# Gated delta layer: merge products on quarters of the array, output and squares as moving operand

## The chip, the cores and the metric

One core of one Trainium2 chip runs one program of eight layers. Its engines are TensorE (PE in the rows; its weight loads are PEld), VectorE (DVE), ScalarE (ACT), GpSimd (POOL) and SyncE (SP), each with its own queue of instructions in program order. They meet at semaphores. The metric is the device time of one execution in microseconds.

## The reference, cut to what matters

The change touches the first layer alone, a gated delta rule with 16 heads (DK = 64, DV = 128), here on 8 batches of 256 tokens, D = 128. T and B of the arrays are set by the inputs.

```python
def _L0_attn_ref(x, w_q, w_k, w_v, w_a, w_b, w_g, w_out, A_log, dt_bias, conv_q, conv_k, conv_v, norm_w):
    q, k, v = x @ w_q, x @ w_k, x @ w_v
    beta = sigmoid(x @ w_b) * 2.0
    g = -exp(A_log) * softplus(x @ w_a + dt_bias)
    q, k, v = (silu(causal_conv4(a, w)) for a, w in ((q, conv_q), (k, conv_k), (v, conv_v)))
    q, k = (a * rsqrt(sum(a * a, -1) + 1e-6) for a in (q, k))          # per head
    def step(S, inp):                                                  # per token and head
        S = S * exp(g_t)
        delta = (v_t - k_t @ S) * b_t
        S = S + outer(k_t, delta)
        return S, (q_t * DK ** -0.5) @ S
    rms = o * rsqrt(mean(o * o, -1) + 1e-5)
    y = rms * norm_w * silu(x @ w_g)
    return y @ w_out                                                   # 2048 -> 128
```

The rest of the network (window attention, Pluecker attention, flash attention, two Mamba scans, four feed-forward blocks) is the same in both kernels.

## The kernel before, in words

`gated_delta` works in chunks of 128 tokens. A quad is one batch with one group of four heads, both chunks (c = 0, 1); there are 8 x 4 = 32 quads. The token recurrence within a chunk becomes a triangular system, whose inverse is built block by block: GpSimd inverts the 16x16 diagonal blocks (`invert`), then three levels of merges double the block, l = 0 (16), l = 1 (32), l = 2 (64). Each merge is two products on TensorE for each chunk, `merge_y` (L1888) and `merge_t` (L1900), four matmuls each, with a copy or masking between them on VectorE (`step_4`, `step_5`, `step_6`) and a copy back on ScalarE (`copy_t`) behind. In between stand small transposes on VectorE (`turn_blocks`, `turn_64`).

The order is written out by hand. Four quads are in flight: `step(x0, x1, x2, x3)` of each engine does the first part of quad x0 (projections, convolution, norms, masked products), pieces of x1, the merges, the solve and the outputs of x2, and the gating and output product of x3. `quads` runs four steps in the body of a loop over the batches, with steps ahead of it and behind it unrolled.

Names used below. `project(x0, n)` (L1821): n = 0 is q, 1 is k, 2 and 3 are v; q and the first half of v go to PSUM bank 4, k and the second half of v to bank 5. ScalarE takes each out of PSUM with the last tap (`tap3`, L2063), VectorE adds the other three taps (`conv`, L2314, six instructions). `sum_squares` (L1838): eight matmuls whose stationary operand is a 128x128 piece of the squares and whose moving operand is `halves` with 2 columns; the sums come out with tokens on partitions, in bank 6. `norms` (L2368 to L2378) on VectorE makes the powers out of them. `out(x3, c)` (L1981): four matmuls per chunk with y as the stationary operand; `add_y` (L2430) on VectorE adds the result from bank 5 into `block_out`. The next projection into bank 5 waits for that add (semaphore `done`).

In the rows each fp32 matmul shows twice ("x16" is eight matmuls), a transpose once. In a step VectorE's order is: masks of level 0, `add_y(x3, 0)`, `conv(x0, 0)`, `step_5`, `conv(x0, 1)`, `turn_64`, `step_6(x2, 0)`, `conv(x0, 2)`, `norms(x0)`, `add_y(x3, 1)`, `step_6(x2, 1)`, `conv(x0, 3)`, then the masked products, `subtract_memory`, `turn_16` and `add_o`, which the next quad's first merge waits for.

## Time and profile before

| | |
|---|---|
| median of 3 runs | 5082.28 us (5075.35 to 5099.08) |
| profiled execution | 5070.0 us, span of the profile 5068.0 us |
| mean granted TensorE clock | 0.896 |
| busy in the span | PE 4077.8 us (80%), DVE 3765.4 (74%), POOL 2812.8 (56%), PEld 2568.3 (51%), ACT 2407.9 (48%) |
| first layer, L1888 (first merge products) | 1536 instructions of 128x64, 188.3 us busy |
| L1900 (second merge products) | 1536 of 128x64, 210.1 us busy |
| L1838 (sums of squares) | 512 of 128x2, 67.7 us busy |
| L1981 (output product) | 512 of 128x128, 75.1 us busy |

The busy times are unions of an engine's instructions. In the rows below, a time ahead of an instruction group is its start in microseconds from the span's start, followed by how long the group lasts; the end of the last matmul of a group is modelled and reaches some 0.2 us past the start of the next. A bracket tells how long the engine sat idle before the group and what ended that. The granted clock is 1.00 at 2.4 GHz and 0.50 at 1.2 GHz.

### The profile page before, as it was taken

To read this page: it belongs to the slowest core of one execution; us is meant where nothing else is said; L and a number is where in the kernel's file an instruction comes from. 1 tells how busy PE (TensorE), PEld (TensorE's weight loads), DVE (VectorE), ACT (ScalarE), POOL (GpSimd) and SP (SyncE) were. 2 spreads that over 40 slices of the span, in tenths; PEclk is the share of its full clock that TensorE was granted. 3 is DMA by queue.
4 is the path that set the end of the run, shared out by engine and by line. 5 is a ranking of instruction groups with operands and counts; after the bars stand their busy time and mean duration, and the time that the engine had idled before them with its cause. 6 is when DMAs were issued, how large, how long until landed. Compare 5 with 4: busy or idle time off the path is not lost. (4 is left out here: it accounts for less than half of the span.)

```text
span 5068.0 us, 74799 instructions
## 1 busy us (share of the span) xinstructions
PE 4077.8 (80%) x19653; PEld 2568.3 (51%) x19773; DVE 3765.4 (74%) x6424; ACT 2407.9 (48%) x4932; POOL 2812.8 (56%) x2705
## 2 busy tenths in 40 slices
PE   5999999999768668667879965688888758888884
PEld 4777777777646546456447742233333323333332
DVE  5676776676567468456138866899999869999995
ACT  3555555555334234222236642566666436666661
POOL 2555555555344144043013330799999529999991
PEclk8999999999877778778999986899999979999997
DMA  1000000000000000000000000000000000000000
GB/s 49 8 8 8 8 8 8 8 7 8 17 0 0 8 13 0 12 1 23 0 17 1 0 13 10 0 0 0 0 0 0 8 0 0 0 0 0 0 0 13
DMA packets 90077, 33.20 MB, mean 7 GB/s; under 512 B 78032, under 2 KB 86112, under 8 KB 88928
## 3 DMA queue, kind: packets, MB, share of 16 engines
q1 hardware_dynamic: 89824, 30.16, 2.5%
q8 instruction: 119, 1.95, 0.2%
q14 instruction: 134, 1.10, 0.1%
HBM read 24.87 MB, written 5.24 MB: 6 GB/s over the span
## 5 line engine op out<-in xcount | busy, mean ns | idle before, releaser
L2970 POOL TENSOR_TENSOR dBx<-dtx,b_row 128x1024 f32<-128x1024 f32 x512 | 1220.4, 2384 | 3.9 <-ACT b_row L2936 3.9
L3004 DVE TENSOR_TENSOR_SCAN h<-banks,dBx 128x1024 f32<-128x1024 f32 x512 | 1168.6, 2283 | 18.1 <-ACT banks L2930 18.1
L2888 PE MATMUL banks<-hc,ident 128*128 128x512 f32 x2048 | 964.6, 594 | 0.0
L2930 ACT ACTIVATE banks<-dt,A 128x510 f32<-128x510 f32 x1024 | 661.7, 682 | 3.6 <-DVE h L3004 3.6
L2936 ACT ACTIVATE b_row<-banks 128x512 f32<-128x512 f32 x512 | 305.9, 597 | 574.1 <-PE banks L2872 574.1
L2888 PEld LDWEIGHTS banks<-hc,ident 128*128 128x128 f32 x2048 | 388.8, 190 | 272.2 <-issue 246.8
L3012 DVE TENSOR_TENSOR hc<-h,banks 128x768 f32<-128x768 f32 x512 | 478.6, 935 | 10.3 <-ACT c_row L2941 6.8
L2872 PE MATMUL banks<-bc_lo,selectors 128*128 128x512 bf16 x1024 | 391.3, 382 | 82.9 <-POOL b_row L2959 73.9
L2979 POOL TENSOR_TENSOR hc<-h,c_row 128x256 f32<-128x256 f32 x512 | 377.0, 736 | 54.5 <-ACT c_row L2941 28.7
L2871 PE MATMUL banks<-bc_hm_c,selectors 128*128 128x512 bf16 x506 | 195.1, 386 | 185.3 <-DVE hc L3012 185.0
L155 POOL MEMSET minus_half<- 128x16 f32 x13 | 1.5, 113 | 520.8 <-POOLq L234 178.8
L2871 PEld LDWEIGHTS banks<-bc_hm_c,selectors 128*128 (+1 forms) x512 | 49.2, 96 | 434.0 <-issue 433.8
L2314 DVE SCALAR_TENSOR_TENSOR v_featmajor<-banks,taps,v_featmajor 128x255 f32<-128x255 f32 (+2 forms) x384 | 167.3, 477 | 130.5 <-ACT v_featmajor L2063 120.0
L2256 POOL TENSOR_TENSOR out_factors<-out_norms,exponents 128x4 f32<-128x4 f32 x64 | 64.5, 1008 | 320.4 <-DVE out_norms L2423 320.4
L821 POOL TENSOR_TENSOR weighted<-probs,f 128x1024 f32<-128x1024 f32 x64 | 120.8, 1904 | 214.8 <-DVE f L872 203.9
L1900 PE MATMUL banks<-inv_turned,steps 128*128 128x64 f32 x1536 | 210.1, 287 | 5.2 <-DVE steps L2339 4.2
L195 PE MATMUL banks<-ident,norm 128*128 128x128 f32 x176 | 45.4, 452 | 209.6 <-DVE norm L165 164.1
L1900 PEld LDWEIGHTS banks<-inv_turned,steps 128*128 128x128 f32 x1536 | 199.2, 203 | 19.5 <-DVE steps L2339 8.7
L1888 PE MATMUL banks<-inv,A_turned 128*128 128x64 f32 x1536 | 188.3, 277 | 24.1 <-issue 19.5
L1888 PEld LDWEIGHTS banks<-inv,A_turned 128*128 128x128 f32 x1536 | 183.2, 196 | 30.9 <-issue 30.9
L2872 PEld LDWEIGHTS banks<-bc_lo,selectors 128*128 (+1 forms) x1024 | 99.6, 97 | 184.0 <-issue 167.0
L2314 DVE SCALAR_TENSOR_TENSOR qk<-banks,taps,qk 128x255 f32<-128x255 f32 (+2 forms) x384 | 167.0, 476 | 23.2 <-ACT qk L2063 12.6
(411 smaller groups left out, 9057.8 us busy)
## 6 DMA issues: line engine op xcount, KB each, us to landing
delta_blocks<-A_turned SPq DMA_DIRECT2D x256, 8.0 KB, 1.5
inv_turned<-delta_blocks SPq DMA_DIRECT2D x256, 8.0 KB, 1.8
blocks<-delta_blocks SPq DMA_DIRECT2D x32, 64.0 KB, 2.1
delta_blocks<-blocks_inv SPq DMA_DIRECT2D x32, 64.0 KB, 1.9
wh<-in_l1f_wh SPq DMA_DIRECT2D x1, 2048.0 KB, 7.6
wqkv<-in_l0f_wqkv SPq DMA_DIRECT2D x2, 768.0 KB, 4.3
residual<-in_x SPq DMA_DIRECT2D x1, 1024.0 KB, 4.7
wv<-in_l0a_wv SPq DMA_DIRECT2D x1, 1024.0 KB, 7.5
```

Of the source, the lines that this page charges most:

```text
L1888: i = mm(k.bank[c][:, h * 64:(h + 1) * 64].rearrange("p (n s) -> p n s", s=s), AT[:, hg, c, h, :], Tm[:, hg % 2, c, h, :].rearrange("p (n ...
L1900: i = mm(k.bank[2 + c][:, h * 64:(h + 1) * 64].rearrange("p (n s) -> p n s", s=s), (step4, step5, step6)[l][:, c, h, :], TT[:, hg % 2, c, ...
L2314: i = stt(out=dst[:, back:], in0=k.bank[4 + n % 2][:, m * T:(m + 1) * T - back], scalar=taps[:, first + m, j:j + 1], in1=dst[:, back:], op ...
L2871: nc.tensor.matmul(k.bank[bank], onto_all(sel[:, 0, bass.ds(n, 1)]), mem[part][:, cols], start=True, stop=False)
L2872: nc.tensor.matmul(k.bank[bank], onto_all(sel[:, which, bass.ds(n, 1)]), mem["lo"][:, cols], start=False, stop=True).then_inc(q[ready], 1)
L2888: i = nc.tensor.matmul(k.bank[e], k.ident[:], hc[:, s, e, :], start=False, stop=False)
L2930: i = nc.scalar.activation(a3[:, :, 1:], d3[:, :, 1:], ACT.Exp, scale=mem["A"][:, e, bass.ds(n, 1)])
L2936: nc.scalar.activation(bsb[:, s, :], k.bank[BBANK], ACT.Copy).then_inc(q["bsb_ready"], 1)
L2970: nc.gpsimd.tensor_tensor(dBx[:, s % NS], dtx[:, :, bass.ds(c * SCH, SCH)], across(bsb[:, s % NS, :], SE), ALU.mult).then_inc(q["dbx_ready ...
L2979: nc.gpsimd.tensor_tensor(hc[:, s % 2, :, DC:], h[:, s % NS, :, DC:], across(csb[:, s % 2, :], SE), ALU.mult).then_inc(q["hcp_ready"], 1)
L3004: v.tensor_tensor_scan(flat(h[:, s % NS]), flat(k.banks[:, at:at + SE, :]), flat(dBx[:, s]), 0.0, ALU.mult, ALU.add).then_inc(q["scanned"], 1)
L3012: v.tensor_tensor(hc[:, s % 2, :, 0:DC], h[:, s, :, 0:DC], across(k.bank[CBANK][:, 0:DC], SE), ALU.mult).then_inc(q["hc_ready"], 1)
```

## The change

Four things. (1) Merge levels 1 and 2 use a part of the array: level 1 two products of 64x64 weights on opposite quarters for each head, with 32 moving columns, level 2 one product of 64x64 weights with 64 columns. The copies on ScalarE shrink to the part that is written, at level 1 in two instructions. (2) The output product has `wout` as the stationary operand and y of both chunks (256 columns) as the moving one. It is done once per quad, summed feature-major over the four quads of a batch in `acc`, then turned by two transposes (`turn_out`) and copied to `block_out` (`copy_out`). (3) `sum_squares` has `halves` as the stationary operand (128 x 8) and the squares as the moving one (256 columns), four matmuls that accumulate. ScalarE copies the 8 x 256 sums (`copy_norms`), and two transposes of TensorE turn them (`turn_norms`); `norms` on VectorE reads the same place as before. (4) The clearing of `block_out` and the filling of two tiles with the identity go, one clearing comes.

The core of the diff:

```diff
-    d["l0a_halves"] = f(row // 64 == np.arange(2)[None, :])
+    d["l0a_halves"] = np.concatenate([f(np.arange(8)[None, :] == 2 * n + row // 64) for n in range(4)], 1)
...
+        def halves_of(a, s):
+            a = a.rearrange("p (n two s) -> p n two s", two=2, s=s)
+            return a[:, :, 0, :], a[:, :, 1, :]
...
                     elif n == 1:
-                        wait(pe, "done", 2 * (qa - LAG - 1) + 1)
+                        if hg == NG - 1:
+                            wait(pe, "yout", b)
...
                     else:
-                        wait(pe, "done", 2 * (qa - LAG))
+                        wait(pe, "done", qa - LAG)
                         wait(pe, "conv", 4 * qa + 2)
...
                     wait(pe, "sq", qa + 1)
                     wait(pe, "Dexp", 2 * qa + 2)
+                    for n in range(4):
+                        i = mm(k.bank[6][0:8, 256:512], halves[:, n, :], sq[:, n, :], start=n == 0, stop=n == 3)
+                    i.then_inc(q["ssfm"], 1)
+
+                def turn_norms(a):
+                    qa = a[0]
+                    wait(pe, "sscp", qa + 1)
+                    pe.sem_inc(q["through_pe"], 1)
                     for c in range(TPB):
-                        for n in range(4):
-                            i = mm(k.bank[6][:, c * 8 + n * 2:c * 8 + n * 2 + 2], sq[:, n, c * P:(c + 1) * P], halves[:],
-                                   start=True, stop=True)
+                        i = tr(k.bank[6][:, c * 8:c * 8 + 8], ssf[:, c * P:(c + 1) * P], k.ident[0:8, 0:8])
                     i.then_inc(q["ssps"], 1)
...
                     for h in range(HG):
-                        i = mm(k.bank[c][:, h * 64:(h + 1) * 64].rearrange("p (n s) -> p n s", s=s), AT[:, hg, c, h, :],
-                               Tm[:, hg % 2, c, h, :].rearrange("p (n two s) -> p n two s", two=2, s=s)[:, :, 0, :],
-                               start=True, stop=True)
+                        cols = slice(h * 64, (h + 1) * 64)
+                        t = Tm[:, hg % 2, c, h, :]
+                        if l == 0:
+                            i = mm(k.bank[c][:, cols].rearrange("p (n s) -> p n s", s=s), AT[:, hg, c, h, :], halves_of(t, s)[0],
+                                   start=True, stop=True)
+                        elif l == 1:
+                            for n in range(2):
+                                r = slice(64 * n, 64 * n + 64)
+                                i = mm(k.bank[c][r, h * 64 + 32 * n:h * 64 + 32 * n + 32], AT[r, hg, c, h, r], t[r, 64 * n:64 * n + 32],
+                                       start=True, stop=True)
+                        else:
+                            i = mm(k.bank[c][64:128, cols], AT[0:64, hg, c, h, 64:], t[0:64, 0:64], start=True, stop=True)
                     i.then_inc(q["Yps"], 1)
...
-                def out(a, e, c):
+                def out(a, x1, e):
                     qe, b, hg = e
-                    wait(pe, "yT", 2 * qe + c + 1)
...
+                    wait(pe, "yT", 2 * qe + 2)
+                    if a is not None:
+                        wait(pe, "conv", 4 * a[0] + 2)
...
                     for h in range(HG):
-                        i = mm(k.bank[5][:, 0:D], yT[:, c, h, :], wout[:, hg * HG + h, :], start=h == 0, stop=h == HG - 1)
+                        i = mm(k.bank[5][:, 0:T].rearrange("p (c t) -> p c t", c=TPB), wout[:, hg * HG + h, :], yT[:, :, h, :],
+                               start=h == 0, stop=h == HG - 1)
                     i.then_inc(q["fin"], 1)
+
+                def turn_out(x1, b):
+                    wait(pe, "done", (b + 1) * NG)
...
+                    for t in range(TPB):
+                        i = tr(k.bank[5][:, t * P:(t + 1) * P], acc[:, t * P:(t + 1) * P], k.ident[:])
+                    i.then_inc(q["yturn"], 1)
...
-                    if x3:
-                        out(x1, x3, 0)
+                    if x3 and x3[2] == 0 and not first(x3):
+                        turn_out(x1, x3[1] - 1)
...
                     if x3:
-                        out(x0, x3, 1)
+                        out(x0, x1, x3)
...
                     if x0:
+                        turn_norms(x0)
                         turn_k(x0)
                         project(x0, 3)
...
+                def copy_norms(a):
+                    qa = a[0]
+                    wait(act, "ssfm", qa + 1)
+                    fn(ssf[:], k.bank[6][0:8, 256:512], ACT.Copy).then_inc(q["sscp"], 1)
...
-                    s = (16, 32, 64)[l]
-                    fn(odd(TT[:, hg % 2, c], s), packed(2 + c, s), ACT.Copy).then_inc(q["TTc"], 1)
+                    if l == 1:
+                        t = packed(2 + c, 32)
+                        fn(TT[0:32, hg % 2, c, :, 32:64], t[0:32, :, 0, :], ACT.Copy)
+                        i = fn(TT[64:96, hg % 2, c, :, 96:128], t[64:96, :, 1, :], ACT.Copy)
+                    else:
+                        i = fn(TT[0:64, hg % 2, c, :, 64:128], packed(2 + c, 64)[0:64, :, 0, :], ACT.Copy)
+                    i.then_inc(q["TTc"], 1)
...
-                def add_y(e, c):
+                def add_y(e):
                     qe, b, hg = e
-                    wait(dve, "fin", 2 * qe + c + 1)
+                    wait(dve, "fin", qe + 1)
+                    y = k.bank[5][:, 0:T]
+                    if hg == 0:
+                        i = vv.tensor_copy(acc[:], y)
+                    else:
+                        i = tt(acc[:], y, acc[:], ALU.add)
+                    i.then_inc(q["done"], 1)
+
+                def copy_out(b):
+                    wait(dve, "yturn", b + 1)
                     dve.sem_inc(q["through_dve"], 1)
-                    y = k.Y[:, bass.ds(b * TPB + c, 1), :].rearrange("p a d -> p (a d)")
-                    tt(y, k.bank[5][:, 0:D], y, ALU.add).then_inc(q["done"], 1)
+                    vv.tensor_copy(k.Y[:, bass.ds(b * TPB, TPB), :].rearrange("p a d -> p (a d)"), k.bank[5][:, 0:T]).then_inc(q["yout"], 1)
```

`merge_t` is changed as `merge_y` is; the rest of the diff repeats these edits in waits and steps.

How the order changes on TensorE from the last merge level to the masked products, in the body of the loop. Before:

```order
L1888 MATMUL banks<-inv,A_turned 128x64 x8
L1900 MATMUL banks<-inv_turned,steps_3 128x64 x4
L1838 MATMUL banks<-halves,squares 128x2 x8
L1924 MATMUL banks<-v,inv_turned 128x128 x4
L1914 MATMUL banks<-wg,x_batch 128x512
L1845 MATMUL banks<-ident,qk 128x128 x2
L1821 MATMUL banks<-norm_featmajor,wv 128x256 x2
```

And of the change, with the semaphores that each waits for:

```order
L1938 MATMUL banks<-inv_turned,steps_3 64x64 x3
L1750 REGISTER_ALU
L1848 MATMUL banks<-squares,halves 8x256 [waits Dexp_3,sq_3]
L1848 MATMUL banks<-squares,halves 8x256 x3
L1750 REGISTER_ALU
L1962 MATMUL banks<-v,inv_turned 128x128 [waits vtok_3,TTc_3]
L1962 MATMUL banks<-v,inv_turned 128x128 x3
L1750 REGISTER_ALU
L1952 MATMUL banks<-wg,x_batch 128x512 [waits conv_3,xb_3]
L1856 MATMUL banks<-ident,norms_featmajor 128x8 [waits sscp_3]
L1856 MATMUL banks<-ident,norms_featmajor 128x8
L1862 MATMUL banks<-ident,qk 128x128 x2
```

The squares are now the moving operand, and two transposes stand behind the gate projection (L1952), where the norms on VectorE get their input.

VectorE between the transposes of the 32-blocks and the convolution of q (`qk`), before:

```order
L2346 TENSOR_TENSOR inv_turned<-banks,inv_turned 128x16x16 [waits TTps_3] x2
L2324 STREAM_TRANSPOSE inv<-inv_turned 32x8x32 x4
L1748 REGISTER_ALU
L2430 TENSOR_TENSOR block_out<-banks,block_out 128x128 [waits fin_3]
L1748 ISA
L2314 SCALAR_TENSOR_TENSOR qk<-banks,taps,qk 128x255 [waits tap3_3]
L2314 SCALAR_TENSOR_TENSOR qk<-banks,taps,qk 128x255
```

And of the change:

```order
L2406 TENSOR_TENSOR inv_turned<-banks,inv_turned 128x16x16 [waits TTps_3] x2
L2384 STREAM_TRANSPOSE inv<-inv_turned 32x8x32 x4
L1750 ISA
L2374 SCALAR_TENSOR_TENSOR qk<-banks,taps,qk 128x255 [waits tap3_3]
L2374 SCALAR_TENSOR_TENSOR qk<-banks,taps,qk 128x255
```

The add, which waits for TensorE's first output product (`fin`), no longer stands ahead of the convolution. The other add of a step keeps its place behind the norms and is now 256 wide; once a batch, `copy_out` stands where the first one stood.

## Rows read from the trace of the kernel before

**Rows 1.** Page, granted clock in 40 slices of the span, tenths

```profile
PEclk8999999999877778778999986899999979999997
```

**Rows 2.** Stretches of the first layer: length, busy time (instructions) by engine, clock

```profile
core 0: us, PE busy (x) PEld busy (x) DVE busy (x) ACT busy (x) POOL busy (x), PEclk, DMA share, GB/s
107.67:1266.54 1158.87, 1057.70 (x6941) 863.15 (x6941) 811.35 (x2322) 594.84 (x1303) 622.87 (x1243) 0.92 0.06 8
704.34:745.45 41.11, 38.16 (x240) 31.02 (x241) 28.07 (x81) 20.53 (x46) 21.59 (x43) 0.88 0.05 8
745.45:785.20 39.75, 36.73 (x241) 30.14 (x241) 28.06 (x81) 20.55 (x46) 21.60 (x43) 0.91 0.05 8
826.56:864.89 38.33, 35.01 (x242) 28.65 (x241) 28.18 (x80) 20.09 (x45) 21.61 (x43) 0.96 0.06 8
810.68:823.31 12.63, 8.97 (x67) 6.91 (x66) 11.89 (x35) 6.18 (x16) 6.12 (x6) 0.97 0.04 4
```

**Rows 3.** The same view, stretches around the sums of squares

```profile
126.40:129.80 3.40, 3.40 (x12) 2.42 (x12) 1.36 (x8) 1.14 (x4) 0.00 (x0) 0.51 0.19 17
841.90:846.30 4.40, 4.40 (x42) 4.40 (x41) 3.04 (x7) 2.37 (x5) 3.06 (x10) 1.00 0.00 0
846.70:850.10 3.40, 3.40 (x11) 2.26 (x11) 1.71 (x8) 1.14 (x4) 1.35 (x2) 0.52 0.16 21
1245.90:1252.70 6.80, 6.80 (x24) 5.30 (x24) 2.10 (x11) 1.53 (x5) 3.80 (x4) 0.50 0.16 22
```

**Rows 4.** TensorE in order of time, one quad: start, length, instructions, idle before

```profile
797.97 1.08 PE L1821 MATMUL banks<-norm_featmajor,wv 128*128 x4
799.55 1.16 PE L1981 MATMUL banks<-wout,y_featmajor 128*128 128x128 f32 x8 [0.50 <-DVE qk L2314]
803.17 1.90 PE L1838 MATMUL banks<-halves,squares 128*128 128x2 f32 x16
...
810.45 1.14 PE L1859 MATMUL banks<-qk 64*128 64x256 f32 x8
811.52 1.13 PE L1940 MATMUL banks<-weighted,k_tokens 128*128 128x256 f32 x4
...
816.35 1.16 PE L1924 MATMUL banks<-v,inv_turned 128*128 128x128 f32 x8
818.21 0.60 PE L1872 MATMUL banks<-ident,v_featmajor 128*128 128x128 f32 x4
...
823.04 2.04 PE L1829 MATMUL banks<-g_masked,tri 128*128 128x512 f32 x2 [3.03 <-issue]
```

**Rows 5.** VectorE in order of time, the same quad

```profile
789.90 1.78 DVE L2324 STREAM_TRANSPOSE inv<-inv_turned 32x256 f32<-32x256 f32 x4
792.49 0.29 DVE L2430 TENSOR_TENSOR block_out<-banks,block_out 128x128 f32 x1 [0.80 <-PE banks L1981]
792.70 2.75 DVE L2314 SCALAR_TENSOR_TENSOR qk<-banks,taps,qk 128x255 f32<-128x255 f32 x6
...
805.11 0.17 DVE L2368 TENSOR_SCALAR norms<-banks 128x16 f32<-128x16 f32 x1 [0.30 <-PE banks L1838]
...
806.52 0.29 DVE L2430 TENSOR_TENSOR block_out<-banks,block_out 128x128 f32 x1
...
810.68 2.76 DVE L2314 SCALAR_TENSOR_TENSOR v_featmajor<-banks,taps,v_featmajor 128x255 f32<-128x255 f32 x6 [3.42 <-ACT v_featmajor L2063]
```

**Rows 6.** ScalarE in order of time, the same quad

```profile
790.41 0.84 ACT L2063 ACTIVATE qk<-banks,taps 128x256 f32<-128x256 f32 x2 [3.14 <-PE banks L1821]
```

**Rows 7.** TensorE in order of time, flash attention: weights of 64 columns

```profile
2657.14 1.15 PE L703 MATMUL banks<-weighted_keymajor,v 128*64 128x128 f32 x16
```

**Rows 8.** Stretches of the Mamba layer (columns as in rows 2)

```profile
3143.70:3147.10 3.40, 2.71 (x7) 0.35 (x5) 2.99 (x6) 0.00 (x0) 0.00 (x0) 1.00 0.00 0
3150.50:3158.00 7.50, 7.50 (x11) 2.82 (x10) 0.00 (x0) 1.97 (x1) 0.00 (x0) 0.50 0.00 0
```

**Rows 9.** Groups by shape, TensorE, 3143.7 to 3147.1: count | busy us, mean ns

```profile
L2712 PE MATMUL banks<-xc,w_xp 128*8 128x512 f32 x4 | 1.9, 593 | 0.0
```

**Rows 10.** TensorE in order of time, 3150.5 to 3158: 8 active rows

```profile
3149.98 9.01 PE L2718 MATMUL banks<-dt_low,w_dt 8*128 8x512 f32 x11
```

More of the change, by code:

```diff
@@ L1716, in gated_delta @@
         tri, hide, ident = p.sb("tri", [P, 2, P]), p.sb("hide", [P, P], BF16), p.sb("ident_bf16", [P, P], BF16)
-        merge, halves, taps = p.sb("merge", [P, 64]), p.sb("halves", [P, 2]), p.sb("taps", [P, 32, 4])
+        merge, halves, taps = p.sb("merge", [P, 64]), p.sb("halves", [P, 4, 8]), p.sb("taps", [P, 32, 4])
         expo = p.sb("exponents", [P, 2 * 2 * HG])
@@ L1735, in gated_delta @@
         gate, yT = p.sb("gate", [P, TPB, HG, DV]), p.sb("y_featmajor", [P, TPB, HG, P])
+        ssf = p.sb("norms_featmajor", [8, T])
+        acc = p.sb("batch_out_featmajor", [P, T])
         sqo, os_, of = p.sb("out_squares", [P, HG, DV]), p.sb("out_norms", [P, TPB, HG]), p.sb("out_factors", [P, TPB, HG])
@@ L1739, in gated_delta @@
                  "xb", "conv", "T16", "Ystep", "TT4", "T32", "T64", "ss", "sp", "AP", "w1", "O1", "osum", "done", "rD", "zeroed",
-                 "inverted", "passed", "passing", "rn", "wd", "y", "there", "back", "through_pe", "through_pool", "through_act", "through_dve")
+                 "inverted", "passed", "passing", "rn", "wd", "y", "yturn", "yout", "ssfm", "sscp", "there", "back", "through_pe", "through_pool", "through_act", "through_dve")
         q = {n: p.sem(n) for n in names}
@@ L1761, in quads, with first @@
                 step(*[at(B - 1, NG + s - n) if n > s else None for n in range(DEPTH)])
+        def first(x):
+            return isinstance(x[1], int) and x[1] == 0
         def even(a, s):
@@ L1898, in merge_t @@
                         wait(pe, "TTc", 4 * qe + c + 1)
+                    pe.sem_inc(q["through_pe"], 1)
                     for h in range(HG):
-                        i = mm(k.bank[2 + c][:, h * 64:(h + 1) * 64].rearrange("p (n s) -> p n s", s=s),
-                               (step4, step5, step6)[l][:, c, h, :],
-                               TT[:, hg % 2, c, h, :].rearrange("p (n two s) -> p n two s", two=2, s=s)[:, :, 1, :],
-                               start=True, stop=True)
+                        cols = slice(h * 64, (h + 1) * 64)
+                        t = TT[:, hg % 2, c, h, :]
+                        if l == 0:
+                            i = mm(k.bank[2 + c][:, cols].rearrange("p (n s) -> p n s", s=s), step4[:, c, h, :], halves_of(t, s)[1],
+                                   start=True, stop=True)
+                        elif l == 1:
+                            for n in range(2):
+                                r = slice(64 * n, 64 * n + 64)
+                                i = mm(k.bank[2 + c][r, h * 64 + 32 * n:h * 64 + 32 * n + 32], step5[r, c, h, r],
+                                       t[r, 64 * n + 32:64 * n + 64], start=True, stop=True)
+                        else:
+                            i = mm(k.bank[2 + c][0:64, cols], step6[64:, c, h, 0:64], t[64:, 64:], start=True, stop=True)
                     i.then_inc(q["TTps"], 1)
@@ L1910, in project_gate @@
                     else:
-                        wait(pe, "yT" if c == 0 else "done", 2 * qe)
+                        if c == 0:
+                            wait(pe, "yT", 2 * qe)
+                        else:
+                            wait(pe, "done", qe)
                     wait(pe, "xb", b + 1)
@@ L1964, in turn_y @@
                         wait(pe, "conv", 4 * a[0] + 1)
+                    else:
+                        wait(pe, "yT", 2 * qe + 1)
                     for h in range(HG):
@@ L2174, in step @@
                         copy_t(x2, 2, 0)
+                    if x0:
+                        copy_norms(x0)
+                    if x2:
                         scale_z(x2, 0)
@@ L2287, in start @@
                 def start():
-                    vv.memset(k.Y[:], 0.0)
                     vv.memset(Tm[:], 0.0)
@@ L2291, in start @@
                     vv.memset(tmp[:], 0.0)
-                    for s in (step5, step6):
-                        vv.tensor_copy(s[:].rearrange("p c h t -> p (c h) t"), across(k.ident[:], TPB * HG))
+                    vv.memset(step5[:], 0.0)
                     dve.drain()
@@ L2444, in step @@
                         turn_blocks(x2, "T32")
-                    if x3:
-                        add_y(x3, 0)
+                    if x3 and x3[2] == 0 and not first(x3):
+                        copy_out(x3[1] - 1)
                     if x0:
@@ L2460, in step @@
                     if x3:
-                        add_y(x3, 1)
+                        add_y(x3)
                     if x2:
@@ L2477, in _ @@
                 quads(dve, step, start)
+                copy_out(B - 1)
 def delta_prologue(k, p, m):
```

17 lines of the change are left out of this document (9 added, 8 removed).

## The prediction

> **What bounds the kernel now.** I read the page's slices first: in the first quarter of the span TensorE's clock stands at 8 to 9 tenths, not at full speed [rows 1]. Then the busy time by stretches [rows 2]. The first layer (the gated delta rule, the only code touched) runs from about 100 to 1305 us in a steady cadence, 29 quads from 107.67 to 1266.54, or 39.96 us each. A quad is the stretch from one start of the first merge product (L1888) to the next. TensorE is busy 91% of it, VectorE 70%.
>
> The same view of three quads shows what makes one quad longer than another. At a granted clock of 0.96 a quad takes 38.33 us, at 0.91 39.75, at 0.88 41.11 [rows 2]. With only the levels 1.0 and 0.5, a mean of 0.96 over 38.33 us is 2 x 0.04 x 38.33 = 3.1 us at the low level; the others are 7.2 and 9.9 us. So 1 us at the low level costs (41.11 - 38.33) / (9.9 - 3.1) = 0.41 us. At 0.92 the mean quad has 6.4 us of it, which costs 2.6 us.
>
> Finer stretches say where the clock is lost [rows 3]. From 841.9 to 846.3 TensorE does not idle at all, yet it issues matmuls of 64 columns (merge products) and of 2 columns (sums of squares); right behind, from 846.7 to 850.1, the clock is 0.52. A low stretch follows this place in all 29 quads, of 3.4 us in 21 of them (the first is at 126.4) and of twice that in 8 (the last is at 1245.9), 4.4 us in the mean. The remaining 2 us per quad lie at the loop's end and at the first merge.
>
> Last, I followed one quad in order of time on TensorE, VectorE and ScalarE [rows 4 to 6]. TensorE waits 0.50 us before the output product at 799.55, for the convolution of k on VectorE, which could not start before the convolution of q had ended (792.70 + 2.75). The quad's second half hangs on VectorE: from 810.68 (the last convolution) to 823.31 it is busy 11.9 of 12.63 us [rows 2]. So whatever starts the last convolution earlier or later moves the quad's end by as much.
>
> **The change, part by part**, as time per quad at the full clock unless said.
>
> (a) Output product. Of two products of 4 matmuls (16 instructions, since each fp32 matmul counts twice in the rows) one of 8 instructions with 256 columns is left. 256 columns cost 0.215 us each (x4 in 1.08 less the last one's tail of 0.2 [rows 4]), so 1.72 us for 2 x 0.98. That alone is 0.2 us. More matters what stood behind it: VectorE waited 0.80 us for the first product (792.49), added, and only then began to convolve q at 792.70. Its input was ready at 791.25 (790.41 + 0.84 on ScalarE [rows 6]) and VectorE free at 791.68 (789.90 + 1.78 [rows 5]). Without the add the convolution starts at about 791.7: both convolutions and all that follows them come 1.0 us earlier. Bounds 0.7 and 1.1.
>
> (b) Merge products on quarters. Level 2: 64 weight columns in place of 128. The nearest row with 64 weight columns takes 16 instructions in 1.15 us [rows 7], 0.06 each after the tail, against 0.11 (x16 in 1.90). Level 1 has twice the instructions, in pairs on opposite quarters. The nearest pairs are the 64-row ones: 8 of 256 columns in 1.07 us (810.45 to 811.52), so two run beside each other. I take 0.5 us for a group of 0.88; bounds 0.44 and 0.88 (no overlap). Of this little reaches the end: level 1 stands between waits for VectorE (the 32-block transposes end at 791.68, the convolution of q after it), and goes into those waits. Level 2, first three groups: 3 x 0.4 = 1.2 us less.
>
> Each visit to a quarter or half of the array costs something at its edges. The four pairs of 810.45 should take 4 x 0.215 = 0.86 and take 1.07: 0.21 per visit, in and out. The Trainium skill, TensorEngine Tiling, Key Properties, says that changing the mode drains the engine; by that alone I would count the visits as here, and the 0.21 agrees. Visits added on the path: level 2, the sums, and the turn of the norms, 0.6 us.
>
> (c) Sums of squares. Before, 16 instructions of 2 columns took 1.90 us less tail, bound by 128-column weight loads. Now 8 instructions with 8 weight columns and 256 moving columns: 8 x 0.215 = 1.72. No gain in time. Together (a) to (c) on TensorE, from the end of k's convolution to the end of the sums: before 5.4 us (799.5 to 803.17 + 1.76), now 1.7 + 0.1 + 1.5 (level 2 with its wait for VectorE's copy) + 0.1 + 1.7 = 5.2. So only the 1.0 us of (a) stands.
>
> (d) The turned sums, the part that costs. The norms on VectorE (L2368 and after) now need a copy on ScalarE (hidden behind the solve and the gate projection, 1.86 us from 816.35 to 818.21) and two transposes that stand behind both. VectorE's chain from the first norm instruction to the add behind it is 1.41 us (805.11 to 806.52 [rows 5]); the add of 256 columns lies between 0.29 (one of 128, 806.52) and 0.46 (one step of the convolution, 2.75 / 6), I take 0.42. And the last projection of v waits for that add ("done"), since it overwrites bank 5. Before, the add ended at 806.81 and the projection came later anyway; now it is late next: transposes 0.3 (four take 0.6, row of 818.21) and their edges 0.2, mode change out of the sums 0.1, handovers 0.15, chain 1.41, add 0.42, exposed first weight load 0.1, less the 0.33 of the k transposes that now hide in the wait = 2.3 us. Behind the waiting projection stand on TensorE the last merge, the k·k products and all that follows; ScalarE's tap and VectorE's last convolution wait for it. Bounds 1.5 (part hidden) and 2.7. TensorE idles about 1.6 us there, a new wait.
>
> (e) The clock. The low stretch behind the sums should go. The mamba layer has both cases [rows 8 to 10]: four matmuls of 512 columns with only 8 weight columns, all 128 rows active, at clock 1.00, and no fall after them; and eleven of 512 columns with 8 active rows, back to back, at 0.50. [...] Gain 4.4 x 0.41 = 1.8 us; bounds 0 and 1.8. But the new wait of (d), with two tiny transposes before it and quarter products behind it, makes a thin stretch of its own two microseconds later. Before the loop's end TensorE waited 3.03 us (823.04), and the clock fell to about half behind it (x2 of 512 columns in 2.04 us; at 0.215 for 256 they would take 0.86, 1.02 with the tail). I give a fall there two chances in three, at 0.9 us (it covers less of the path): +0.6. Bounds 0 and 2.8 (two low stretches). The Trainium skill, TensorE: Matmul & The Clock Gate, section "Why this matters for your kernels", asks for no idle gaps of microseconds between bursts. By that rule a wait of 1.6 us harms nothing, this term is 0 and the time 5067. The rows are against it as a sufficient rule: the fall of rows 3 had no gap before it.
>
> (f) Once a batch, the sum is turned and copied out: 0.43 us on VectorE ahead of q's convolution, 0.1 us per quad. The removed clearing of block_out (1.8 us once) and the end's extra turn (1.5 us) cancel. The split copies on ScalarE (+0.2) fall into its waits.
>
> **Sum.** Per quad -1.0 + 2.3 - 1.8 + 0.6 + 0.1 = +0.2, times 30 quads = +6 us, within what I can resolve here. Against the profiled execution (5068.0 us span, 5070 with what lies around it) that is 5076. The median of the runs lies 12 us higher, 5082.28; some of that is chance, and I say 5085.
>
> **Rivals.**
> *Clock gain outweighs (faster).* The wait behind the norms stays at its low bound (1.5) or the clock never falls there: -1.0 + 1.5 - 1.8 + 0.3 + 0.1 = -0.9, or 27 us: about 5050. For it: 91% busy TensorE, the 0.41 us slope, the 8-column rows. Against it: the chain of 1.41 + 0.42 us is on the rows and cannot overlap the transposes. Down to 5025 if both happen.
> *The low stretch only moves (slower).* The new wait at the turned norms gives the clock away every quad as the squares did before, one or two stretches: -1.0 + 2.3 - 1.8 + 1.8 + 0.1 = +1.4, times 30 = +42 us: about 5125. It decides from about nine falls in ten quads. For it: halved merge products leave TensorE fewer streamed columns elsewhere too, with short waits for VectorE between them. Against it: a stretch of full-rate sums, solve and gate stands right before the wait.
> *Level 1 does not overlap.* 32 instructions a level at 0.055 are then as long as before; they end in waits, at most 0.2 us per quad, 5090. This I count with the forecast.
>
> **How the numbers follow.** No change: 0.40 (5060 to 5110 as its own range). Faster by the clock: 0.31. Slower: 0.29. A measurement of this kernel tells about 0.5% (25 us) from nothing. The chances of the three signs are those of the cases. The range runs from 5030 to 5135, short of both rivals' ends.
>
> **What would show it.** The stretch behind the sums should have a granted clock near 1.0 where it was 0.52. VectorE's convolution of q should start without waiting for TensorE's output product. The last projection of v (now L1832) should show a wait for VectorE of 1 to 2 us, ended by the add into batch_out_featmajor. Level-2 groups should take about 0.5 us for 8 instructions. If the new sums do not hold the clock, or if the projection does not wait, the forecast is wrong in (e) or (d).

## The result: 0.9% slower, inside the range, by the rival and not by the forecast

| | before | after |
|---|---|---|
| median on the same chip | 5077.21 us (5064.55 to 5099.08, 8 runs) | 5123.88 us (5115.25 to 5127.13, 8 runs) |
| ratio | | 1.0086, 95% interval 1.0068 to 1.0103 |
| profiled execution: time, span, clock | 5070.0, 5068.0 us, 0.896 | 5117.39, 5115.5 us, 0.896 |
| first 28 quads | 39.97 us each, clock 0.92 | 42.36 us each, clock 0.90 |

The time lies in the range (5030 to 5135), 39 us from the 5085 forecast and 1 us from the rival "the low stretch only moves" (5125, chance 0.29). The forecast was no change. The loss of 0.86% is clear of its interval, so that part of it is wrong, although the range held. One of the seven executions of e8_merges_only below was slow, 7606.73 us, and does not enter its ratio.

The same view as [rows 2] of the changed kernel. First the 28 quads, then one quad, then two stretches of it, ahead of and behind the turned norms:

```profile
106.38:1292.32 1185.94, 990.37 (x7226) 717.88 (x7225) 802.50 (x2221) 594.12 (x1342) 601.08 (x1200) 0.90 0.05 8
866.00:907.70 41.70, 34.83 (x259) 25.03 (x259) 28.44 (x79) 20.84 (x48) 21.60 (x43) 0.92 0.05 7
884.00:889.50 5.50, 3.69 (x20) 1.87 (x18) 2.98 (x11) 1.90 (x6) 4.27 (x7) 1.00 0.11 18
889.90:896.70 6.80, 6.80 (x25) 4.67 (x26) 4.04 (x12) 1.58 (x4) 1.82 (x1) 0.50 0.05 6
```

TensorE works less than before (a quad of 41.70 us holds 34.83 us of matmuls; before, one of 39.75 us held 36.73 [rows 2]) and is slower all the same. The clock is 1.00 through the sums, where it was 0.52 behind them [rows 3]. But right behind the new wait it is 0.50 for 6.8 us, where before the low stretch behind the sums lasted 4.4 us in the mean. Such a fall, of one or more stretches of 3.4 us, follows that place in 25 of 28 quads.

TensorE in order of time in that quad, answering to [rows 4]:

```profile
879.39 1.99 PE L2019 MATMUL banks<-y_featmajor,wout 128*128 128x256 f32 x8 [0.99 <-DVE qk L2374]
881.31 1.14 PE L1916 MATMUL banks<-inv,A_turned 64*64 64x64 f32 x16
882.69 0.65 PE L1938 MATMUL banks<-inv_turned,steps 64*64 64x64 f32 x8 [0.24 <-DVE steps L2422]
883.27 1.89 PE L1848 MATMUL banks<-squares,halves 128*8 128x256 f32 x8
885.09 1.16 PE L1962 MATMUL banks<-v,inv_turned 128*128 128x128 f32 x8
...
887.04 0.29 PE L1856 MATMUL banks<-ident,norms_featmajor 8*128 8x8 f32 x2
887.26 0.44 PE L1862 MATMUL banks<-ident,qk 128*128 128x128 f32 x2
889.78 1.92 PE L1832 MATMUL banks<-norm_featmajor,wv 128*128 x4 [2.09 <-DVE batch_out_featmajor L2492]
891.64 1.11 PE L1938 MATMUL banks<-inv_turned,steps 64*64 64x64 f32 x8
892.68 2.08 PE L1876 MATMUL banks<-qk 64*128 64x256 f32 x8
894.69 2.07 PE L1978 MATMUL banks<-weighted,k_tokens 128*128 128x256 f32 x4
```

The wait stands where it was forecast, at the last projection, and is ended by the add into `batch_out_featmajor`. Behind it each group takes nearly twice its time: the products (L1876) 2.08 us where [rows 4] has 1.14 for the same shape, the state (L1978) 2.07 for 1.13. VectorE in the same quad, answering to [rows 5]:

```profile
870.71 1.79 DVE L2384 STREAM_TRANSPOSE inv<-inv_turned 32x256 f32<-32x256 f32 x4
872.52 2.76 DVE L2374 SCALAR_TENSOR_TENSOR qk<-banks,taps,qk 128x255 f32<-128x255 f32 x6
...
887.37 0.18 DVE L2428 TENSOR_SCALAR norms<-banks 128x16 f32<-128x16 f32 x1 [2.12 <-PE banks L1856]
...
889.22 0.42 DVE L2492 TENSOR_TENSOR batch_out_featmajor<-banks,batch_out_featmajor 128x256 f32<-128x256 f32 x1
889.67 0.43 DVE L2422 COPY steps<-banks 64x256 f32<-64x256 f32 x1
892.71 2.76 DVE L2374 SCALAR_TENSOR_TENSOR v_featmajor<-banks,taps,v_featmajor 128x255 f32<-128x255 f32 x6 [2.61 <-ACT v_featmajor L2112]
```

The first convolution starts without waiting for TensorE. The chain from the norms to the end of the add takes 2.27 us (887.37 to 889.64). It waits 2.12 us for the turned sums, and two things that wait for nothing but VectorE stand behind it: the add (its product was done at 881.4) and the last step of the merges.

**A part of the loss is hidden in the span.** The layer itself is 72.6 us longer, 1433.9 us for 1361.3 from its first to its last matmul, yet the span grew by 47.5. The unchanged layer behind it gave 22.3 us of that back. Its first window attention before, and after:

```profile
1411.20:1707.40 296.20, 230.59 (x1249) 181.37 (x1249) 195.88 (x367) 123.08 (x345) 120.89 (x58) 0.75 0.00 1
```

```profile
1484.30:1758.20 273.90, 203.74 (x1249) 159.93 (x1249) 198.58 (x367) 123.40 (x345) 121.29 (x58) 0.86 0.00 1
```

The instructions and their counts are equal, the clock is 0.75 and 0.86. In the profiles of the runs below the same code took 280.8 to 293.5 us, so the two kernels compared here stand at the two ends of 14 profiles, and the others lie between. I take it for no property of the change, which one profile of each kernel cannot prove.

### The profile page after: what moved, and what is told of

It is laid out like the page before. It is cut to its first block and busy times, and to the rows that moved or that the text cites. A ratio compares the mean times of both kernels' runs of the same rounds, so it can differ in the third digit from the quotient of the medians.

```text
span 5115.5 us, 76210 instructions
## 1 busy us (share of the span) xinstructions
PE 4018.3 (79%) x20365; PEld 2407.3 (47%) x20365; DVE 3787.3 (74%) x6398; ACT 2430.3 (48%) x5028; POOL 2810.9 (55%) x2705
## 3 DMA queue, kind: packets, MB, share of 16 engines
q14 instruction: 135, 1.11, 0.1%
## 5 line engine op out<-in xcount | busy, mean ns | idle before, releaser
L2940 PE MATMUL banks<-bc_hm_b,selectors 128*128 128x512 bf16 x512 | 196.4, 384 | 77.2 <-POOL b_row L3028 73.1
L2940 PEld LDWEIGHTS banks<-bc_hm_c,selectors 128*128 (+1 forms) x512 | 49.2, 96 | 434.1 <-issue 433.9
L203 ACT ACTIVATE norm_featmajor<-banks 128x512 f32<-128x512 f32 x48 | 28.4, 598 | 294.0 <-PE banks L195 294.0
L1490 POOL TENSOR_TENSOR squares<-qkv_ahead 128x1024 f32<-128x1024 f32 x32 | 61.0, 1906 | 172.9 <-ACT qkv_ahead L1426 172.9
L2294 POOL TENSOR_TENSOR blocks_inv<-blocks_inv,block_products 64x14 f32<-64x14 f32 (+6 forms) x448 | 117.8, 263 | 63.7 <-issue 0.3
```

Of the source, the lines that this page charges most:

```text
L2294: i = tt(U[:, 0:j, j + 1:], U[:, 0:j, j + 1:], tmp[:, 0:j, 0:n], ALU.add)
L2940: nc.tensor.matmul(k.bank[bank], onto_all(sel[:, 0, bass.ds(n, 1)]), mem[part][:, cols], start=True, stop=False)
```

## The experiments

Three theories. **A**: the place of the norms' chain on VectorE makes the wait, and the half clock behind it follows from the wait. **B**: the quarters cost it. **C**: sums with 8 weight columns, and their small transposes, bring the clock down wherever they stand. Ratios are to the kernel before on the same chip, with 95% intervals. Its median was 5077 us beside the first four, 5069 beside the next seven and 5061 beside the last.

| run | what | median, us | ratio |
|---|---|---|---|
| e1_add_first | after, add ahead of norms | 5048.77 | 0.9942 (0.9928 to 0.9957) |
| e2_add_step_first | and step_6 ahead too | 4987.90 | 0.9830 (0.9816 to 0.9844) |
| e3_old_sums | after, old sums | 5036.79 | 0.9917 (0.9894 to 0.9940) |
| e4_sums_only | before, new sums | 5125.19 | 1.0095 (1.0078 to 1.0112) |
| e5_fill_wait | after, 7 idle products in the wait | 5090.89 | 1.0039 (1.0021 to 1.0058) |
| e6_old_sums_order | e3 in the order of e2 | 5038.52 | 0.9927 (0.9904 to 0.9950) |
| e7_out_only | before, new output product | 5063.38 | 0.9986 (0.9972 to 0.9999) |
| e8_merges_only | before, quarters | 5050.15 | 0.9946 (0.9924 to 0.9968) |
| e9_fill_four | after, 4 idle products | 5055.36 | 0.9965 (0.9950 to 0.9980) |
| e10_whole_order | e2, merges on the whole array | 5008.98 | 0.9875 (0.9853 to 0.9897) |
| e11_gate_behind | e2, gate projection later | 4983.15 | 0.9835 (0.9811 to 0.9859) |
| e12_sums_order | e4 in the order of e2 | 5006.53 | 0.9887 (0.9867 to 0.9907) |

**e1 and e2, the order on VectorE.** e1 moves `norms` behind `add_y`, e2 behind `step_6` as well:

```diff
                         conv(x0, 2)
-                        norms(x0)
                     if x3:
                         add_y(x3)
                     if x2:
                         step_6(x2, 1)
+                    if x0:
+                        norms(x0)
```

> The changed kernel with one edit: on VectorE the add of the output product (0.42 us) stands ahead of the norms' chain of quad's first part, and no longer behind it. Theory A (the place of the turned norms: TensorE waits 2.09 us at the last projection of v for the add, which stands behind a chain that itself waits for the turned sums, and the two stretches at half the clock follow from that wait): the wait at the last projection falls from 2.1 us to under 0.5, the third convolution starts 1 to 1.5 us earlier in its quad, a quad takes 40.3 to 41.2 us in place of 42.35, and the time is 5065 to 5095. Theory B (products on quarters of the array cost their mode changes and bring the clock down by themselves): the wait goes, but the low stretch stays and the quad stays at 42 us, 5110 to 5130. Theory C (sums with 8 active rows bring the clock down wherever they stand): as B, 5105 to 5130, with the low stretch right behind the sums or the transposes.

> As the run before, and also the last step of the merges (step_6 of the second half) stands ahead of the norms' chain on VectorE. Theory A: as the run before or up to 0.3 us per quad better, since nothing that TensorE waits for stands behind the norms any more: 5055 to 5090; if the norms then come late for the weighted keys, a new wait of some 0.5 us on the norms shows and it is 5080 to 5100. Theories B and C: 5105 to 5130.

Both were faster than theory A said. The groups on TensorE, count | busy us, mean ns | idle ahead, over the first 28 quads, of the changed kernel:

```profile
L1876 PE MATMUL banks<-qk 64*128 64x256 f32 x448 | 84.2, 507 | 1.5 <-DVE QK_turned L2452 1.5
L1832 PE MATMUL banks<-norm_featmajor,wv 128*128 (+1 forms) x224 | 74.4, 463 | 60.3 <-DVE batch_out_featmajor L2492 41.7 <-DVE batch_out_featmajor L2490 18.1
L1978 PE MATMUL banks<-weighted,k_tokens 128*128 128x256 f32 x112 | 54.5, 638 | 0.0
L1938 PE MATMUL banks<-inv_turned,steps 64*64 64x64 f32 x448 | 47.0, 261 | 6.6 <-DVE steps L2422 4.8
```

of e1:

```profile
L1876 PE MATMUL banks<-qk 64*128 64x256 f32 x448 | 65.2, 409 | 0.0
L1832 PE MATMUL banks<-norm_featmajor,wv 128*128 (+1 forms) x224 | 61.2, 396 | 0.1
L1938 PE MATMUL banks<-inv_turned,steps 64*64 64x64 f32 x448 | 37.7, 226 | 49.2 <-DVE steps L2422 47.4
L1978 PE MATMUL banks<-weighted,k_tokens 128*128 128x256 f32 x112 | 37.3, 463 | 0.0
```

and of e2:

```profile
L1876 PE MATMUL banks<-qk 64*128 64x256 f32 x448 | 63.5, 400 | 22.4 <-DVE QK_turned L2452 22.4
L1832 PE MATMUL banks<-norm_featmajor,wv 128*128 (+1 forms) x224 | 61.0, 395 | 0.1
L1938 PE MATMUL banks<-inv_turned,steps 64*64 64x64 f32 x448 | 37.0, 222 | 5.3 <-DVE steps L2422 3.3
```

In e1 the wait did not go. It moved one group on, from 60.3 us at the projection to 49.2 us at the last merge, since the last step of the merges still stood behind the norms. Yet these four groups were busy 58.7 us less (201.4 for 260.1), the clock over the 28 quads was 0.96 for 0.90, and the fall behind this place came in 7 quads of 28. So most of e1's gain is the clock (the sums per quad are in the part on the prediction). In e2 the second wait goes too, the fall comes in none of 28, and 61 us more come out. What is left is 22.4 us for the decayed scores, which the kernels with the old sums have as well (20.2 us in e3, 14.3 us in the kernel before).

**e5 and e9, the clock apart from the wait.** The wait stays, TensorE only streams through it:

```diff
                         turn_k(x0)
+                        x = k.HT[:, bass.ds(x0[1], 1), PAD:].rearrange("p a t -> p (a t)")
+                        for n in range(7):
+                            mm(k.bank[2][:, 256:512], wv[:, 0:P], x, start=True, stop=True)
                         project(x0, 3)
```

(`range(4)` in e9). They are called idle since nobody reads what they write.

> The changed kernel with seven idle products (128x256, on the whole array, into bank 2, which nobody reads then) put between the turning of k and the last projection of v, in the 2.09 us that TensorE waits there. Nothing else moves. They take about 1.8 us, the length of the wait, so the place of the add is not mended; only TensorE streams through the wait. From the first two runs: taking the wait away at this place left a wait of 50.7 us in 29 quads two lines later (the last merge), about as long, and the time still fell by 75 us. Theory A1 (most of what the change cost is the half clock that follows the wait): the low stretches behind the wait go, a quad falls from 42.35 us to 39.5 to 41, and the time is 5040 to 5080. Theory A2 (the wait itself, some 2 us in 28 quads, is the cost): the clock rises but the time stays within 15 us of 5124, or rises by what the products overhang.

> The fifth run with four idle products in place of seven. Seven took 3.19 us there (one is issued as two instructions of 0.23 us), 1.1 us more than the wait of 2.09 that they were to cover; four take 1.8 us and fit in. Theory A1 (the half clock behind the wait is the larger part of the loss): a further 0.8 to 1.1 us per quad against the fifth run, ratio to the kernel before 0.996 to 1.000, so 5045 to 5070 beside 5069. Theory A2 (the wait's own length is the cost and the fifth run's gain is chance): ratio 1.005 to 1.009, 5095 to 5120.

TensorE in e9, one quad in order of time:

```profile
689.44 0.29 PE L1856 MATMUL banks<-ident,norms_featmajor 8*128 8x8 f32 x2
689.66 0.44 PE L1862 MATMUL banks<-ident,qk 128*128 128x128 f32 x2
689.93 1.89 PE L2076 MATMUL banks<-norm_featmajor,wv 128*128 x8
692.18 1.10 PE L1832 MATMUL banks<-norm_featmajor,wv 128*128 x4 [0.35 <-DVE batch_out_featmajor L2495]
693.21 0.67 PE L1938 MATMUL banks<-inv_turned,steps 64*64 64x64 f32 x8
693.82 1.13 PE L1876 MATMUL banks<-qk 64*128 64x256 f32 x8
694.88 1.13 PE L1978 MATMUL banks<-weighted,k_tokens 128*128 128x256 f32 x4
```

The projection still starts 2.5 us after the k transposes began (692.18 - 689.66), as in the changed kernel (889.78 - 887.26). Behind it nothing is slow any more: 1.10, 0.67, 1.13 and 1.13 us, where the changed kernel takes 1.92, 1.11, 2.08 and 2.07. Useless work made the kernel 1.2% faster (0.9965 against 1.0086, 61 us), faster than the kernel before. So theory A1 holds: the half clock was worth more than the whole loss of 0.86%. Seven products were my slip in size. They take 3.19 us in e5, overhang the wait by 1.1, and cost 36 us against four, so that e5 (5091) missed the range of both its cases.

The Trainium skill, page TensorE: Matmul & The Clock Gate, section "HAM oscillation — how this bites in real kernels", gives as its abstract rule that TensorE should have no idle gaps of more than several microseconds. The trace goes further: behind an idle time of about 2.1 us the clock fell in 25 of 28 quads. When it was streamed through, the clock fell in 2 of 28.

**e3 and e6, the old sums.** e3 takes back `halves`, the 16 products of two columns, and drops the copy and the turning. e6 adds the order of e2.

> The changed kernel with the sums of squares as before (16 products with two columns each, nothing turned); quarters and the new output product stay. Theory A: the wait and the two low stretches go with the turning; what is left is the output product's -1.0 us and the quarters' +0.6 us per quad, so 39.6 us per quad and 5055 to 5075, with a low stretch of 4 to 6 us per quad left where it was before. Theory B: the quarters are what costs, so it stays at 5105 to 5130. Theory C: 5055 to 5080, like A.

> The kernel of the third run (old sums, quarters, new output product) with the order of the second (add and last step of the merges ahead of the norms' chain on VectorE). Theory A (the order matters only since the norms' chain waits for the turned sums): no turned sums, nothing to gain: 5025 to 5045, as the third run with 5037; and the new sums, once in the right order, are worth 35 to 60 us (second run 4988). Rival (the order is the gain and the sums give nothing): 4980 to 5000.

e3 was faster than any of its cases. The medians of e6 and e3 are equal: without turned sums the order is worth nothing in time. The profiles show more. In e6 a quad has 7.74 us at the half clock and in e3 4.82, and without what that costs it would be 0.7 us shorter in e6, so the order may gain something there that the clock takes back. Theory B falls as the whole cause, since with the quarters in and the new sums out the kernel is 0.8% faster than before.

**e4 and e12, the new sums alone.**

```diff
-                    for c in range(TPB):
-                        for n in range(4):
-                            i = mm(k.bank[6][:, c * 8 + n * 2:c * 8 + n * 2 + 2], sq[:, n, c * P:(c + 1) * P], halves[:],
-                                   start=True, stop=True)
+                    for n in range(4):
+                        i = mm(k.bank[6][0:8, 256:512], halves[:, n, :], sq[:, n, :], start=n == 0, stop=n == 3)
...
                     if x0:
+                        turn_norms(x0)
                         turn_k(x0)
```

> The kernel before with the new sums alone (8 active rows, q and k squared streaming, copied and turned). Merges on the whole array and the output product with one half each as before. Theory A: the turning costs 1.5 to 2.7 us per quad as in the changed kernel, less what the low stretch behind the sums gives back: 5100 to 5135. Theory B: 5065 to 5085, no slower than before. Theory C: 5100 to 5135; A and C part in the first two runs.

> The fourth run's kernel (the kernel before with the new sums alone, ratio 1.0095) with the second half's add and the last step of the merges ahead of the norms' chain on VectorE. Theory A (the new sums cost time only where the add stands behind their chain; by themselves they take the low stretch away): ratio 0.985 to 0.993, 4995 to 5035 beside 5070. Rival (they gain only together with the quarters and the new output product): 0.998 to 1.005, 5060 to 5095.

Two kernels with the same instructions in another order on one engine lie 2.1% apart (1.0095 and 0.9887). The stretch of 28 quads of e4:

```profile
105.15:1286.69 1181.54, 1020.69 (x6534) 795.46 (x6533) 804.24 (x2242) 585.24 (x1286) 599.48 (x1200) 0.94 0.05 8
```

and of e12:

```profile
105.24:1178.00 1072.76, 973.59 (x6534) 767.55 (x6533) 799.34 (x2242) 583.91 (x1286) 599.62 (x1200) 0.97 0.06 8
```

At the same count of matmuls TensorE is busy 47 us less at the clock of 0.97. The other 62 us of the 109 are idle time, and at the last projection alone e4 waits 59.8 us and e12 none. Theory C falls: the 8-column sums and the 8-row transposes are in e12 too.

e4 has nearly the same wait at the same place as the changed kernel (a median of 2.08 us for 2.09), but the clock fell behind it in 13 quads of 28, not in 25, and a quad has 5.43 us at the half clock for 8.60. So the wait alone does not decide it: the quarters and the new output product, which e4 leaves out, together have a share in the falls. With this wait in place they gained nothing in all (1.0095 without them, 1.0086 with them).

**e7, e8 and e10, the other two parts.** e7 has the output product alone, e8 the quarters alone, e10 is e2 without the quarters. The core of e8's edit, which e10 takes back:

```diff
-                        i = mm(k.bank[c][:, h * 64:(h + 1) * 64].rearrange("p (n s) -> p n s", s=s), AT[:, hg, c, h, :],
...
+                        elif l == 1:
+                            for n in range(2):
+                                r = slice(64 * n, 64 * n + 64)
+                                i = mm(k.bank[c][r, h * 64 + 32 * n:h * 64 + 32 * n + 32], AT[r, hg, c, h, r], t[r, 64 * n:64 * n + 32],
+                                       start=True, stop=True)
+                        else:
+                            i = mm(k.bank[c][64:128, cols], AT[0:64, hg, c, h, 64:], t[0:64, 0:64], start=True, stop=True)
```

> The kernel before with the output product alone changed (wout as the matrix that stays, both halves in one, sums kept transposed and turned once per batch). The prediction's term (a): -1.0 us in each of 30 quads with (f) +0.1, so 5045 to 5055. Rival (the third run's -40 us comes from the quarters): 5070 to 5085.

> The kernel before with the second and third level of the merges on quarters of the array alone. The prediction's term (b): +0.6 us in each of 30 quads, with bounds of 0.44 and 0.88 us on a group of products: 5085 to 5105. Rival (the third run's gain comes from the quarters, whose four small products ran in 0.53 us a group and level 3 at 64 columns in 1.1): 5040 to 5065.

> The kernel of the second run (ratio 0.983) with the merges back on the whole array; new sums, new output product and the mended order stay. It prices the quarters where TensorE has no low stretch to win back. If they give what they save in TensorE's time (80 us less busy over 29 quads in the run with the quarters alone, of which 27 us of time came out): ratio 0.988 to 0.995, 5010 to 5045. If their gain in that run came only through the clock: 0.981 to 0.986, as the second run.

In none of the three did the first case hold. e7 (5063) lies between its two cases, e8 (5050) came out as its rival, and e10 (0.9875) lies between its cases. For e7 and e8 the reason is that I took the prediction's terms (a) and (b) out one by one. They belong together: (c) sums TensorE's time behind k's convolution over all three, and e8's expectation kept (b)'s cost of the visits and left out its 1.2 us less at level 2. The output product alone gave 0.14% (7 us). VectorE in e7:

```profile
666.01 1.78 DVE L2346 STREAM_TRANSPOSE inv<-inv_turned 32x256 f32<-32x256 f32 x4
668.36 2.77 DVE L2336 SCALAR_TENSOR_TENSOR qk<-banks,taps,qk 128x255 f32<-128x255 f32 x6 [0.56 <-ACT qk L2086]
...
675.22 0.43 DVE L2379 STREAM_TRANSPOSE inv<-inv_turned 32x256 f32<-32x256 f32 x1
678.11 0.43 DVE L2384 COPY steps<-banks 64x256 f32<-64x256 f32 x1 [2.46 <-PE banks L1898]
```

The convolution of q starts 0.57 us after the transposes end, where it was 1.02 (791.68 to 792.70 [rows 5]): 0.45 us won, since ScalarE's tap is late next in this quad. But the whole product now stands between k's convolution and level 2. The wait for level 2's product is 2.46 us, and it was 1.62 in the quad of [rows 5]: 0.84 us lost. Over the first 28 quads the convolution of q starts 0.44 us behind the transposes in the mean, where it was 1.45, and the wait for level 2's product is 2.45 us a quad for 1.65. So the 1.0 us forecast in (a) was won, and 0.8 us of it was lost one convolution later.

The quarters alone gave 0.54% (27 us). Alone they took about 78 us of TensorE's busy time in 28 quads out of the merges (266 us for 344 us in the groups of both merge products). Part of it went into waits for VectorE's convolutions, and part into the clock: at 8.10 us of half clock per quad for 6.76 the profiled execution of e8, 14 us above the median, has the same quads as the kernel before (39.95 and 39.97 us). The wait at the transposes of y:

```profile
L1989 PE MATMUL banks<-ident,v 128*128 128x128 f32 x220 | 38.4, 301 | 40.8 <-DVE qk L2341 32.5 <-POOL v L2290 8.3
```

It is 40.8 us, where the kernel before waits 24.5. At e10 against e2 the quarters are worth 0.45% with the order mended, about as much as alone.

**e11, one move more.**

```diff
                         solve(x2, 0)
-                        project_gate(x0, x2, 0)
...
                         project(x0, 3)
+                        project_gate(x0, x2, 0)
```

> The kernel of the second run with one more move: on TensorE the gate's first projection (1.0 us) goes behind the last projection of v. In the second run's trace the third convolution starts when ScalarE has copied that projection, and at the second products TensorE waits 0.76 us for the product of decay and scores behind it. If that chain sets the end there, the wait goes: 0.5 to 0.8 us per quad, ratio 0.977 to 0.981, 4955 to 4975. If the next wait (the state, or the transposed v) takes its place: 0.982 to 0.985, no change.

No change, the rival's case. The wait for the decayed scores falls from 22.4 to 4.2 us, and 13.9 us come at the next one:

```profile
L1962 PE MATMUL banks<-v,inv_turned 128*128 128x128 f32 x448 | 64.2, 286 | 13.9 <-DVE v L2462 13.9
L1876 PE MATMUL banks<-qk 64*128 64x256 f32 x448 | 63.2, 398 | 4.2 <-DVE QK_turned L2452 4.2
```

e2 and e11 beat both kernels, by 1.7% and 1.6% against before. Within their intervals they are the same.

## Where the prediction held and where it failed, step by step

With the 0.41 us per us of low clock that the prediction read from three quads, a mean quad splits into a length at full clock and what the clock adds. The low time per quad, time at a granted clock of 0.50, is taken from the clock's record over the first 28 quads (the mean clock gives about the same: twice the missing share times the length, 2 x 0.10 x 42.36 = 8.5 us in the changed kernel). It is 6.76 us before, 8.60 after, 4.82 in e3, 2.22 in e9, 2.14 in e12 and 2.39 in e2; the quads are 39.97, 42.36, 38.76, 39.81, 38.31 and 37.53 us long. At full clock that makes 37.2, 38.8, 36.8, 38.9, 37.4 and 36.6. The slope can be tested: after and e9 do the same work, differ by 6.38 us of low time and by 2.55 us in length, 0.40. This pair bears it out. Each length comes from one profiled execution, and e3's was 20 us faster than its median (5017.23 and 5036.79).

| step | forecast, per quad | measured |
|---|---|---|
| (a) to (c) and (f) at full clock | -1.0 + 0.1 = -0.9 | -0.4 (36.8 less 37.2) |
| (d) turned sums at full clock | +2.3 | +2.0 (38.8 less 36.8) |
| (e) clock | -1.8 + 0.6 = -1.2 | +0.75 (8.60 less 6.76, times 0.41) |
| sum | +0.2 | +2.4 (42.36 less 39.97) |

**The views and the mechanism of (a) to (d) held.** The wait came where it was put (2.09 us for "about 1.6", with its releaser), the convolution of q ran free, level 2's groups took 0.57 us a group (1.14 for two), and the new sums took 1.8 us to the start of the next group. At full clock (a) to (c) with (f) saved 0.5 us per quad less than forecast, and (d) cost 0.3 less. What was too low is the time from the end of k's convolution to the end of the sums: the prediction has 5.2 us for it (its terms add up to 5.1), and the quad above takes 5.70 (879.39 to 885.09), where the kernel before took 5.4. e3 is 42 us faster than before, which is 1.4 us per quad, but part of that is its shorter low time, which the forecast of (a) to (c) did not have.

**(e) was the step that failed**, by 2.0 of the 2.2 us per quad between forecast and measurement. Its first half was right: the low stretch behind the sums goes, and it is worth what was said. e12 has the new sums without the wait: at full clock it is near the kernel before (37.4 and 37.2), its low time is 4.6 us shorter, and by its ratio it is 57 us faster, 1.9 us per quad against the 1.8 forecast (1.7 between the two profiles). The second half was mis-sized. I gave the new wait "two chances in three, at 0.9 us". The clock fell behind it in 25 quads of 28, and mostly for two stretches rather than one. That is 6.0 us of low time per quad, 2.4 us at the slope, where the forecast had 0.6. The low clock also fell on the products and the state, which are on the path: the time lost per us of it was no smaller there (0.40), though I had assumed so ("it covers less of the path"). The upper bound of the term, 2.8 us for two stretches, was the nearer end. The rows had shown the direction: 3.03 us of waiting at the loop's end with a fall behind it [rows 4]. I discounted it for the full-rate work standing ahead.

**The median is nearer to the forecast than the step is, and that is luck.** 2.4 us in 30 quads is 72 us. The spans of the profiled executions differ by 47.5, mostly since the unchanged window attention ran at 0.86 instead of 0.75. That the time came out 1 us from the rival's 5125 owes as much to this: the rival had the mechanism, but at +1.4 us per quad. How much of it stands in every run is open: only one execution of each kernel was profiled.

**Not looked at in the prediction:** that the cost of (d) was an order on VectorE. I listed the add and the last step of the merges as standing behind the chain, and priced the queue as given. Neither needs the norms. With both ahead of it, the same change is 1.7% faster than before.

**Open.** In e1 a wait of about 1.4 us, one projection later, was followed by a fall in only 7 quads, and in e4 a wait as long as the changed kernel's, at the same place, in 13. What in the work around a wait decides this was not separated; no run varied the length of the wait at a fixed place without also changing what stands beside it.

## What to carry to other kernels

When a step turns into a chain across engines, look at what stands behind its last link in the in-order queue of each engine: work that is ready and has someone waiting for it goes ahead. Price a new wait on TensorE twice, once for its length and once for the clock behind it. Which is larger depends on the rest of the kernel. Between the changed kernel and e2 a quad lost 4.8 us, 2.5 of them by the clock (6.21 us of low time at 0.41). Between e4 and e12 it lost 3.9 us, and 1.3 by the clock. A few idle products in the wait are a cheap way to tell the two apart.

## What the runs showed of the hardware

- Idle matmuls can pay: four products of 128x256 in a wait of 2.09 us raised the mean clock of 28 quads from 0.90 to 0.97 and took 1.2% off the time. The stretch of e9:

```profile
107.70:1222.32 1114.62, 965.68 (x7449) 707.19 (x7449) 800.42 (x2221) 593.86 (x1342) 599.48 (x1200) 0.97 0.05 8
```

- Less work on TensorE was no protection: with the quarters alone the low time per quad grew from 6.76 to 8.10 us, though TensorE's busy time fell by 44 us in 28 quads.
- The same code of 1249 matmuls took 273.9 us at a clock of 0.86 and 296.2 us at 0.75, with no change in it.
